# Attention values on half chunks of 64 keys and eight array tiles, Q half behind the scores, z turned in two places

## The reference

```
q = norm(x) @ Wq + bq;  k, v = ctx @ Wk + bk, ctx @ Wv + bv      # 16 heads of 32
attn = softmax(clip(q @ k.T * 32**-0.5, -10000, 10000))          # 77 keys a head
x = x + (attn @ v) @ Wo + bo
H = gelu((norm(x) @ U1) @ V1 + b1)                               # 512 -> 128 -> 2048
x = x + (H @ U2) @ V2 + b2                                       # 2048 -> 128 -> 512
```

## Time and profile before

| what | before |
|---|---|
| median of 3 runs | 610.51 us |
| the profiled execution | 610.8 us |
| its span | 608.9 us |
| TensorE busy | 581.9 us, 96% |
| VectorE busy | 488.9 us, 80% |
| GpSimd busy | 358.1 us, 59% |
| ScalarE busy | 309.6 us, 51% |
| values matmuls (L1019) | 51.9 us, 800 records |
| scores matmuls (L970) | 36.2 us, 1024 records |
| turns of probabilities (L996) | 49.9 us, 320 records |
| normalising on GpSimd (L394) | 72.1 us, 32 instructions |
| mean granted clock of TensorE | 0.989 |

### The profile page before, as it was taken

One profiled execution on the slowest core, in us unless ns is written; L12 is line 12 of the kernel. 1 busy time (PEld: TensorE's weight loads), 2 busy tenths in 40 slices (PEclk: granted clock), 3 DMA queues, 4 the chain that ended last, 5 costly groups with the idle time before them and its releaser, 6 DMA issues.

```text
span 608.9 us, 11499 instructions
## 1 busy us (share of the span) xinstructions
PE 581.9 (96%) x4583; PEld 478.9 (79%) x4583; DVE 488.9 (80%) x706; ACT 309.6 (51%) x505; POOL 358.1 (59%) x250
## 2 busy tenths in 40 slices
PE   6988899999999999999999897999999999999996
PEld 5786888888888888888886666878888888888884
DVE  3489878797879787988768986697979797978675
ACT  1435254445444444444445553565757575757562
POOL 2548575657565756675666535565656665656561
PEclk8989899999999999999999999999999999999999
DMA  8423064122312221222122134003030302001012
GB/s 263 153 66 110 20 211 142 39 97 88 104 40 84 87 105 47 78 87 71 53 104 71 53 122 172 2 18 122 34 104 36 104 36 103 36 36 52 18 52 86
DMA packets 29746, 50.31 MB, mean 83 GB/s; under 512 B 5069, under 2 KB 6783, under 8 KB 29567
## 3 DMA queue, kind: packets, MB, share of 16 engines
q1 hardware_dynamic: 29215, 48.80, 23.6%
q10 hardware_dynamic: 480, 0.80, 0.6%
HBM read 32.49 MB, written 16.78 MB: 81 GB/s over the span
## 4 chain that ended last, share of the span: by engine, by line
PE 78%; DVE 9%; DMA 4%; ACT 3%; issue 2%; POOL 2%; SPq 1%; DVEq 0%; ACTq 0%; POOLq 0%
PE bank L922 44%; PE ps_s L922 14%; PE bank L1019 6%; PE bank L996 5%; PE ps_s L970 4%; PE bank L1043 2%; DVE ssum L723 2%; PE bank L944 2%; DMA fw<-in_L_xattn_Wk 2%; DVE smax L718 1%; DMA xs<-in_x 1%; DMA fw<-y_between 1%; DVE ss L709 1%; PE ps_s L1087 1%; DVE once L762 1%
## 5 line engine op out<-in xcount | busy, mean ns | idle before, releaser
L454 POOL TENSOR_TENSOR hs_r<-ss,hs_r 128x512 fp32r<-128x512 f32 x63 | 89.7, 1424 | 93.2 <-ACT hs_r L622 92.7
L601 ACT ACTIVATE ss<-ps_s,bias_c 128x512 f32<-128x512 f32 x128 | 88.1, 689 | 69.3 <-PE ps_s L922 65.7
L387 POOL TENSOR_TENSOR ss<-ss,smax 128x1232 f32<-128x1232 f32 x32 | 75.0, 2344 | 70.7 <-DVE smax L718 70.7
L922 PE MATMUL ps_s<-p1t_r,v_r 128*128 128x512 f32 x384 | 113.3, 404 | 0.6 <-DVE p1t_r L774 0.6
L922 PE MATMUL bank<-hs_r,u_r 128*128 128x512 f32 x384 | 110.2, 396 | 1.4 <-DVE hs_r L785 1.4
L922 PE MATMUL bank<-zt_r,wqo_r 128*128 128x256 f32 x768 | 100.7, 287 | 0.4 <-DVE zt_r L661 0.4
L922 PE MATMUL bank<-wqo_r,ot_r 128*128 128x512 f32 x384 | 97.7, 403 | 0.2 <-DVE xs L741 0.2
L922 PEld LDWEIGHTS bank<-zt_r,wqo_r 128*128 128x128 f32 x768 | 94.5, 191 | 1.6 <-issue 1.0
L394 POOL TENSOR_TENSOR ss<-ss,rsum 128x1232 f32<-128x1232 f32 x32 | 72.1, 2252 | 39.2 <-DVE rsum L725 39.2
L922 PEld LDWEIGHTS bank<-hs_r,u_r 128*128 128x128 f32 x384 | 72.4, 189 | 19.3 <-DVE hs_r L785 2.3
L922 PEld LDWEIGHTS ps_s<-p1t_r,v_r 128*128 128x128 f32 x384 | 70.6, 190 | 15.6 <-DVE v_r L748 1.1
(11 more groups left out here) (89 smaller groups left out, 855.6 us busy)
## 6 DMA issues: line engine op xcount, KB each, us to landing
xs<-in_x SPq DMA_DIRECT2D x64, 256.0 KB, 3.1
y_between<-xs SPq DMA_DIRECT2D x32, 256.0 KB, 2.0
xs<-y_between SPq DMA_DIRECT2D x4, 1024.0 KB, 5.5
fw<-y_between SPq DMA_DIRECT2D x4, 1024.0 KB, 5.4
out<-xs SPq DMA_DIRECT2D x16, 256.0 KB, 2.0
out<-fw SPq DMA_DIRECT2D x16, 256.0 KB, 2.0
ss<-in_L_xattn_Wq SPq DMA_DIRECT2D x2, 512.0 KB, 10.8
xs<-in_L_xattn_Wo SPq DMA_DIRECT2D x1, 1024.0 KB, 11.0
```

What stands on the lines that cost most here:

```text
L387: pool.tensor_tensor(heads(sc, k), heads(sc, k), smax[:, k, :].unsqueeze(2).broadcast_to([P, H, KV]), ALU.subtract).then_inc(s_sub, 1)
L454: pool.tensor_tensor(hs[:, c % 4, 1, :], hg[:, c % 4, :], hs[:, c % 4, 0, :].bitcast(F32), ALU.subtract)\
L601: act.activation(hg[:, c % 4, :], ps_s[:, c % 4, :], ACT.Gelu_apprx_tanh, bias=b1_c[:, c:c + 1]).then_inc(h_gelu, 1)
L922: mm = pe.matmul(ps, lhs(a), rhs(c), start=first and i == 0, stop=last and i == len(PASSES) - 1)
```

## The change

**Layout of the probabilities.** `normalise` no longer works in place. It reads `sc` (now two slots of 1232 columns) and writes `sn` (two slots of 1280): first the 64 first keys of each of the 16 heads, so that a chunk of 128 holds exactly two heads, one in each half of the rows after the turn; then, in the last two chunks, the last 16 keys of each head (keys 61 to 76), ordered so that the four heads of one group stand in one half chunk. It is two instructions. Nothing is filled up with zeros.

**Values.** `vrows` has a part 0 (64 rows by 32 columns for each head) and a part 1, in which the 13 last keys of a head stand in the last 13 of its 16 rows, and zeros in all others. 10 DMAs place it. `weigh_values` has 32 matmuls of 64 rows by 32 columns against 256 moving columns: two for each head, on eight tiles (two halves of the rows, four columns). Row half 0 writes B5, row half 1 B6. There is one signal at the end, and the whole set waits for `zt_lo`.

**Order.** On TensorE (and ScalarE's copies with it) `project_q` half 0 goes right behind the scores of tile 0, ahead of the turns of probabilities. `project_out` of tile 0 goes ahead of `turn_probs` part 2; that of tile 1 goes between the two z turns. VectorE's `y_sum` of tile 1 goes between the two `turned_z`.

**Waits.** The clip waits for the normalising of two tiles earlier; `normalise` waits for the turns of two tiles earlier; the first gelu waits for the last normalising, since its output lies over `sc`.

The core of the diff:

```diff
-            for q, (h, c) in enumerate(PIECES):
-                p0, kv0, n = piece_rows(h, c)
-                sp.dma_start(vrows[p0:p0 + n, :, q, :],
-                             v_f[kv0:kv0 + n, :, head_at(h) * DH:(head_at(h) + 1) * DH]).then_inc(v_placed, 16)
-                if q == NP // 2:
-                    load_x(2, 0)
+            for r in range(2):
+                sp.dma_start(vrows[r * HALF:(r + 1) * HALF, 0, :, :, :, :].rearrange("p b e i d -> p (b e i d)"),
+                             v_f[0:HALF, r, :, :, :].rearrange("p b e d -> p (b e d)")).then_inc(v_placed, 16)
+            load_x(2, 0)
+            v_heads = v_f.rearrange("p r b e (i d) -> p r (b e) i d", i=GH)
+            for r in range(2):
+                for i in range(GH):
+                    p0 = r * HALF + (i + 1) * TAIL - (KV - HALF)
+                    sp.dma_start(vrows[p0:p0 + KV - HALF, 1, :, :, i, :].rearrange("p b e d -> p (b e) d"),
+                                 v_heads[HALF:KV, r, :, i, :]).then_inc(v_placed, 16)
...
             def normalise(j, b, u):
+                k, s = 2 * b + u, 2 * num(j, b) + u
+                pool.wait_ge(s_rec, s + 1)
+                until(pool, pt_full, 3 * (s - 1))
+                pool.tensor_tensor(sn[:, u, 0:H * HALF].rearrange("p (h w) -> p h w", h=H), heads(u)[:, :, 0:HALF],
+                                   rsum[:, k, :].unsqueeze(2).broadcast_to([P, H, HALF]), ALU.mult)
+                grouped = lambda t: t.rearrange("p (i g) w -> p i g w", i=GH)
+                pool.tensor_tensor(sn[:, u, H * HALF:].rearrange("p (g i w) -> p i g w", g=G, i=GH),
+                                   grouped(heads(u)[:, :, KV - TAIL:KV]),
+                                   grouped(rsum[:, k, :].unsqueeze(2).broadcast_to([P, H, TAIL])),
                                    ALU.mult).then_inc(s_norm, 1)
...
             def heads_high(j, b):
                 n = 2 * j + b
+                act.wait_ge(pv_full, n + 1)
                 for half, bk_ in ((0, B5), (1, B6)):
-                    act.wait_ge(pv_full, 2 * n + half + 1)
...
             def clip(j, b, u):
-                until(dve, pt_full, 3 * (s - 3))
+                until(dve, s_norm, s - 1)
...
                     if there(NA, j, b, 2):
-                        turned_z(j + 1, b)
+                        turned_z(j + 1, b, (0,))
+                    if there(NA, j, b, -2):
+                        y_sum(j - 1, b, 1)
+                    if there(NA, j, b, 2):
+                        turned_z(j + 1, b, (1,))
...
             def weigh_values(j, b):
                 pe.wait_ge(pt_copied, 6 * n + 6)
-                for half, bk_ in ((0, B5), (1, B6)):
-
-                    if half and (not isinstance(j, int) or n + 3 < NA):
-                        pe.wait_ge(zt_lo, 2 * (n + 3) + 1)
-                    for i in range(2):
-                        for head, q, c, first, final in value_steps(2 * half + i):
-                            d0 = head * DH
-                            last = pe.matmul(bk_[d0:d0 + DH, i * TA:(i + 1) * TA], vrows[:, b, q, :],
-                                             pt[:, c, :], start=first, stop=final)
-                    last.then_inc(pv_full, 1)
+                if there(NA, j, b, 3):
+                    pe.wait_ge(zt_lo, 2 * (n + 3) + 1)
+                for e in range(2):
+                    for part in range(2):
+                        for i in range(GH):
+                            c = 2 * GH + e if part else 2 * i + e
+                            for r, bk_ in ((0, B5), (1, B6)):
+                                rows = slice(r * HALF, (r + 1) * HALF)
+                                last = pe.matmul(bk_[i * DH:(i + 1) * DH, e * TA:(e + 1) * TA],
+                                                 vrows[rows, part, b, e, i, :], pt[rows, c, :],
+                                                 start=part == 0, stop=part == 1)
+                last.then_inc(pv_full, 1)
...
                         if here:
                             scores(j, b, u)
+                        if u == 0 and after:
+                            project_q(*shift(j, b, 1), 0)
                         if before:
                             turn_probs(*shift(j, b, -1), u, (0, 1))
...
+                        if u == 0 and there(NA, j, b, -2):
+                            project_out(j - 1, b, 0)
+                        if u == 1 and after:
+                            project_q(*shift(j, b, 1), 1)
                         if before:
                             turn_probs(*shift(j, b, -1), u, (2,))
-                            project_out(j - 1, b, u)
...
                     if there(NA, j, b, 2):
-                        turn_z(j + 1, b)
+                        turn_z(j + 1, b, (0,))
+                    if there(NA, j, b, -2):
+                        project_out(j - 1, b, 1)
+                    if there(NA, j, b, 2):
+                        turn_z(j + 1, b, (1,))
```

More of the change, by code:

```diff
@@ L27 @@
 SCALE = DH ** -0.5
[L29 to L37, removed]
+HALF = P // 2
+TAIL = HALF // GH
 TA = 256
@@ L594, in gelu @@
                 act.wait_ge(h_full, n + 1)
+                if is_block(0, j, b) and c == 0:
+                    act.wait_ge(s_norm, 2 * NA)
                 if not isinstance(j, int) or n >= 4:
@@ L654, in norm_z, with turned_z @@
                                       ALU.subtract, ALU.mult).then_inc(z_done, 1)
-            def turned_z(j, b):
+            def turned_z(j, b, us=(0, 1)):
                 n = 2 * j + b
-                for u in range(2):
+                for u in us:
                     bk_ = z_bank(j, b, u)
@@ L697, in _, with heads @@
             v_sum(1)
[L699 to L701 removed]
             turned_z(0, 1)
             def clip(j, b, u):
[L706 removed]
+                s = 2 * (2 * j + b) + u
                 dve.wait_ge(s_full, s + 1)
[L708 to L709 removed]
+                until(dve, s_norm, s - 1)
+                dve.tensor_scalar(sc[:, u, :].rearrange("p (g w) -> p g w", g=G), ps_s[:, :, 0:GW],
                                   CLAMP, -CLAMP, ALU.min, ALU.max).then_inc(s_clip, 1)
[L712 to L713 removed]
+            def heads(u):
+                return sc[:, u, :].rearrange("p (h w) -> p h w", h=H)
             def maxima(j, b, u):
@@ L924, in product, with turn_z @@
                 return mm
-            def turn_z(j, b):
+            def turn_z(j, b, us=(0, 1)):
                 n = 2 * j + b
-                for u in range(2):
+                for u in us:
                     bk_ = z_bank(j, b, u)
@@ L996, in turn_probs @@
                         last = pe.transpose(bk_[:, (c % 4) * P:(c % 4 + 1) * P],
-                                            sc[:, k, c * P:(c + 1) * P], ident[:, :])
+                                            sn[:, u, c * P:(c + 1) * P], ident[:, :])
                     last.then_inc(pt_full, 1)
-            def value_steps(g):
-                mine = [[(q, c) for q, (hh, c) in enumerate(PIECES) if hh == i * G + g] for i in range(GH)]
-                for k in range(max(len(m) for m in mine)):
-                    for head, m in enumerate(mine):
-                        if k < len(m):
-                            yield head, *m[k], k == 0, k == len(m) - 1
             def weigh_values(j, b):
@@ L1130, in body @@
                             scores(j, b, u)
+                        if u == 0 and after:
+                            project_q(*shift(j, b, 1), 0)
                         if before:
-                            if isinstance(j, int) and num(j, b, -1) == 0 and u == 0:
-                                pe.wait_ge(pad_zero, 1)
                             turn_probs(*shift(j, b, -1), u, (0, 1))
@@ L1139, in body @@
                             hidden(0, 0, 1)
-                        if after:
-                            project_q(*shift(j, b, 1), u)
+                        if u == 0 and there(NA, j, b, -2):
+                            if is_block(2, j, b):
+                                pe.wait_ge(wo_lo, 1)
+                                pe.wait_ge(zt_lo, 8)
+                            project_out(j - 1, b, 0)
+                        if u == 1 and after:
+                            project_q(*shift(j, b, 1), 1)
                         if before:
                             turn_probs(*shift(j, b, -1), u, (2,))
-                        if there(NA, j, b, -2):
-                            if isinstance(j, int) and num(j, b, -2) == 0 and u == 0:
-                                pe.wait_ge(wo_lo, 1)
-                                pe.wait_ge(zt_lo, 8)
-                            project_out(j - 1, b, u)
                         if is_block(NA, j, b) and u == 0:
```

62 lines of the change are left out of this document (26 added, 36 removed).

## The result

| | before | after |
|---|---|---|
| median of the runs compared | 610.80 us (609.56 to 611.31) | 592.61 us (591.75 to 593.30) |
| profiled execution | 610.8 | 592.9 |
| its span | 608.9 | 591.1 |
| TensorE busy, of the span | 96% | 94% |

The changed kernel takes 0.9708 of the time [0.9688 to 0.9728], 18 us less. (This median of the kernel before is over four executions, the 610.51 us of the forecast over three of them.) The forecast was 596.6 us with a range from 593 to 605.

A forecast was written before the change was run, and what follows sets the result against it. TensorE's queue, busy 96% of the span, was taken as the bound. Steady blocks 11.5, opening 0.5, passage 1.4 and end 0.6 sum to 14.0 us off the 608.9 us span, giving 596.6 us; range 593 to 605.

The forecast's parts named there:

- The values: Values matmuls on TensorE: set falls from 3.22 to 1.94 us, 1.31 us less per block.
- The cheap end: Values set: all eight array tiles run side by side, saving 1.31 us per block.
- rivals 2 and 3: Values set: row halves take turns, 617 us, chance 0.11; or eight tiles overlap only in part, 604 us, chance 0.08.
- The steady block: TensorE's block in tile pairs 3 to 12: 20.09 becomes 18.8 us, nine blocks saving 11.5 us.
- The opening: Stretch before the steady blocks: 0.5 us saved, bounds 0 and 2.5, fourth values set at 120.1 against 120.62.
- the long block: Block 3 in the opening: 21.8 us instead of 18.8, its values held by the late x tile.
- The clip of (1,1): VectorE in the opening: this clip waits for the normalising of (0,1), 0.65 us late, on a full chain.
- The trap: Block 3: x load, issued behind feed-forward weights and y's store, still lands at 94.6, so the block takes 21.8 us.
- VectorE: Steady block: its 16.8 us of work fits in 18.8; first z low part ends at +17.8, one microsecond to spare.
- The moves: Steady block: Q half behind the scores removes a 0.1 us wait; the wait for z's low part is hidden.
- Passage: Into the feed-forward part: first block 1.4 us less, the next two blocks nothing saved.
- after the last values: TensorE's wait for `ot` at 361.41: 0.6 us less, with the copies 0.65 earlier.

The follow-up runs named there:

- The order alone: The kernel before with the new order of Q half, output projections and z turns but the old values matmuls; 604.92 us, 0.9908.
- weights and turns together: Changed kernel with feed-forward weight loads spread over blocks 4 to 10 and 16 unused turns ahead of the first values; 588.82 us, 0.965.
- both parts and the weights spread together: Changed kernel with feed-forward weight loads spread, an own slot for tile (1,1)'s scores, and 16 unused turns before the first values; 587.99 us, 0.9635.

## Why the prediction was right, and what it missed

- **The values.** Right: a set of 1.96 us against 1.94, a saving of 1.26 per block against 1.31. The cheap end holds and rivals 2 and 3 fell with it. The Trainium skill (TensorE: Matmul & The Clock Gate, section "Wait — 56ns, not 53.3ns?") has about 62 ns per matmul without hardware decode. The prediction counted that by records and got 4 us for 64 of them; they take 1.96, 0.031 each, so counted so it doesn't hold here. But the 64 records are 32 matmuls of the program, 0.061 us each (the scores, two records each as well, 0.056), and no run shows whether hardware decode was off, so the rule itself is neither shown nor refuted.
- **The steady block, a term that was too small.** I wrote "20.09 - 1.31 - 0.1 + 0.1 (one more change between turns and projection, each way) = 18.8". No row stood behind the last term. The order alone took 0.17 off the block (20.10 to 19.93), where I had it at nothing. The extra change does show at one place (two turns to the scores behind them, 0.31 us, where two turns to the projection were 0.14), but the set of eight turns behind Q half 0 takes 0.79 to its follower, where the set behind the scores took 0.91, and other steps got shorter too. With 1.26 + 0.16 = 1.42 per block the nine give 12.80, 1.3 over the forecast.
- **The opening, the step that failed most.** I wrote "0.5 us, bounds 0 and 2.5"; it was 2.53. The fourth set came at 118.09 instead of 120.1. Of these 2.0 us, 1.05 were there at 28 us, ahead of all changed TensorE work: scores (0,0) start at 28.74 against 29.79, since the same 24 matmuls of the K projection took 3.38 us, at a granted clock of 1.00, against 4.97 us, with a granted clock of 0.50 from 11.4 to 14.8. In later runs of other kernels with this code unchanged they took 3.38 to 6.31, so this is luck of the execution. A term for this has no place in a sum, but it belonged in the range. Another 0.5 is the first block, 20.08 against 20.6: half speed ended at 60.7, and the scores behind the set ran at 1.13. The other 0.4 is the long block (21.50 against 21.8) and the steady one behind it (18.68 against 18.8). The count is of one execution: the other three had a lower granted clock, 0.986 against 0.990, and took 592.31, 591.75 and 593.30 us against its 592.9.
- **The clip of (1,1).** The wait came as priced (0.58 against 0.65) but not on the path: taking it away changed no distance, and z ended 0.28 us behind GpSimd's subtraction with and without it.
- **The trap.** Right in place, cause and size: x at 92.56, 14.65 us behind the second values set (15.1 written), with 3.67 us of waiting, a block of 21.50, and 2.82 of it gone when the weights came later.
- **VectorE.** Right: clips at +4.64 and +11.72 against +4.9 and +12.0, the first z low part from +16.94 to +17.60 against +17.2 to +17.8, and no wait in any steady block.
- **The moves.** The order's worth was weighed as if the old set were there: 0.1 and "hidden". With the short set, each covers a wait of over 1 us. The number was not touched, since both are in the change, but "nothing is late" hid how much hangs on them.
- **Passage.** -1.4 and 0 held (1.42, 0.31); after the last values 0.74 against 0.6.
- **The range.** Its low end was called the good bound of the opening, 2.5 us. That gives 594.6; the further 1.6 us down to 593 were tied to no term. The opening came out at that bound (2.53), and the steady blocks, the passage and the end took 1.3 + 0.3 + 0.1 us more. Had either the opening or the steady term come as forecast, the time would lie inside. Nothing was allowed for how executions of one kernel differ, 4.0 us in the four of weights and turns together.

## What to carry to other kernels

Here a shorter burst of matmuls paid only when what was made under its cover was made earlier too. So list, for each operand of the burst and of what follows, when it is ready against the new start. Order matmuls for array tiles so that neighbours in the queue lie on different tiles. After a gain, look for the transfers that were hidden by the time now saved.

## What the runs showed of the hardware

Eight array tiles of 64 by 32 work side by side as four of 128 by 32 do: the records of one tile follow each other every 0.216 us for 256 fp32 columns in both, and the second row half comes free. What I had not expected is the dependence on order: with one row half queued ahead of the other, 2.85 us instead of 1.96 for the same records. Nor that kernels whose TensorE code is the same up to there start their first scores between 28.74 and 31.06 us: the K projection takes 3.38 us where the granted clock is 1.00 throughout, some 5 us where it is 0.50 for part of it (11.4 to 14.8 us in the kernel before), and 6.16 where it is 0.50 up to 16.9 us (both parts and the weights spread together). For the latest start, 31.06, behind a projection of 6.31, the trace has no clock before 17.5 us.
